# A unit's probability planes turned by four DMA transposes of 32 rows instead of one of 128

## What is computed

```python
xn = _layernorm(x, ln_gamma, ln_beta)
q = (xn @ w_q).reshape(B, SQ, NUM_HEADS, DIM_HEAD)
k, v = jnp.split(context @ w_kv, 2, axis=-1)        # context: 32 x 1500 x 128
...
scores = jnp.einsum('bqhd,bkhd->bhqk', q * SCALE, k)
attn = jax.nn.softmax(scores, axis=-1)
out = jnp.einsum('bhqk,bkhd->bqhd', attn, v).reshape(B, SQ, INNER)
out = out @ w_out + b_out
return out * jnp.tanh(gate[0])
```

## Time and profile before

| | us |
|---|---|
| median of 3 runs | 2121.29 (2121.03 to 2125.9) |
| the profiled execution, its own time | 2123.42 |
| its span, first to last instruction | 2121.6 |
| first and last issue of a transpose of this stage | 716.8, 1909.5 |

### The profile page before, as it was taken

One profiled execution on the slowest core, in us unless ns is written; L12 is line 12 of the kernel. 1 busy time (PEld: TensorE's weight loads), 2 busy tenths in 40 slices (PEclk: granted clock), 3 DMA queues, 4 the chain that ended last, 5 costly groups with the idle time before them and its releaser, 6 DMA issues. The chain is left out here.

```text
span 2121.6 us, 32242 instructions
## 1 busy us (share of the span) xinstructions
PE 1753.3 (83%) x9613; PEld 1229.7 (58%) x9613; DVE 1557.0 (73%) x2744; ACT 1153.5 (54%) x1804; POOL 821.0 (39%) x687
## 2 busy tenths in 40 slices
PE   4877886999844589989988988998898898884997
PEld 3554555888712446656655665665565566453886
DVE  4884775787755478778777877877777787775887
ACT  2432222776621566666666665666666576563453
POOL 4650111233333463444346345434533634411233
PEclk9987998899956799999999999999999999997998
DMA  5102774000000499899989989998998998882000
GB/s 203 50 0 94 292 287 189 2 1 0 1 0 30 99 197 193 182 189 188 188 185 192 195 176 189 188 193 187 191 192 170 199 192 183 180 167 87 1 9 10
DMA packets 722858, 290.11 MB, mean 137 GB/s; under 512 B 700892, under 2 KB 705020, under 8 KB 722044
## 3 DMA queue, kind: packets, MB, share of 16 engines
q1 hardware_dynamic: 722796, 289.36, 59.9%
HBM read 112.24 MB, written 0.92 MB: 53 GB/s over the span
## 5 line engine op out<-in xcount | busy, mean ns | idle before, releaser
L2147 DVE TENSOR_REDUCE xa_negmax<-xa_psum 128x1 f32<-128x1500 f32 x224 | 385.4, 1720 | 219.2 <-PE xa_psum L2055 219.2
L2265 ACT ACTIVATE xa_h<-xa_psum,xa_rinv 128x1000 f16<-128x1000 f32 x448 | 372.1, 881 | 236.1 <-DVE xa_rinv L2154 144.1
L2162 DVE SCALAR_TENSOR_TENSOR xa_h<-xa_psum,xa_rinv,xa_h 128x500 f16<-128x500 f32 x672 | 452.8, 729 | 55.3 <-ACT xa_h L2265 55.3
L2253 ACT ACTIVATE xa_psum<-xa_psum,xa_negmax 128x1500 f32<-128x1500 f32 x224 | 332.6, 1485 | 195.0 <-DVE xa_negmax L2147 195.0
L2053 PE MATMUL xa_psum<-xa_c_hi,xa_q_hi 128*128 128x500 f32 x672 | 293.2, 436 | 143.9 <-DVE xa_h L2162 134.7
L2073 PE MATMUL xa_psum<-xa_prT,xa_n_hi 128*128 128x512 f16 (+1 forms) x768 | 278.1, 362 | 5.5 <-DMA xa_prT<-xa_h 3.2
L2074 PE MATMUL xa_psum<-xa_prT,xa_n_hi 128*128 128x512 f16 (+1 forms) x768 | 274.4, 357 | 0.0
L2075 PE MATMUL xa_psum<-xa_prT,xa_n_lo 128*128 128x512 f16 (+1 forms) x768 | 273.0, 356 | 0.0
L2055 PE MATMUL xa_psum<-xa_c_hi,xa_q_lo 128*128 128x500 f32 x672 | 271.3, 404 | 0.0
L2054 PE MATMUL xa_psum<-xa_c_lo,xa_q_hi 128*128 128x500 f32 x672 | 270.5, 403 | 0.0
L2053 PEld LDWEIGHTS xa_psum<-xa_c_hi,xa_q_hi 128*128 128x128 f32 x672 | 131.5, 196 | 231.5 <-DVE xa_h L2162 183.9
(11 more groups left out here) (296 smaller groups left out, 3373.5 us busy)
## 6 DMA issues: line engine op xcount, KB each, us to landing
ctxN<-in_ctxP SPq DMA_DIRECT2D x16, 1536.0 KB, 9.3
xa_ctxP<-in_ctxP SPq DMA_DIRECT2D x32, 768.0 KB, 4.8
ctxT<-in_ctxT SPq DMA_DIRECT2D x16, 1500.0 KB, 6.3
xa_ctxT<-in_ctxT SPq DMA_DIRECT2D x32, 750.0 KB, 4.7
xa_prT<-xa_h SPq DMA_TRANSPOSE x224, 5.5
up<-in_F_up SPq DMA_DIRECT2D x1, 2048.0 KB, 9.2
down<-in_F_down SPq DMA_DIRECT2D x1, 2048.0 KB, 13.3
gate<-in_F_gate SPq DMA_DIRECT2D x1, 1024.0 KB, 4.9
```

The costliest lines, as they stand in the source:

```text
L2147: nc.vector.tensor_reduce(negmax[:, s % 2, :], psum[:, bank:bank + 3, 0:W], AX.XY, ALU.max, negate=True)\
L2162: nc.vector.scalar_tensor_tensor(h[:, H_SLOT[s], 1, a:z], psum[:, bank + j, 0:W], rinv[:, s % 2, :], h[:, H_SLOT[s], 0, a:z], ALU.mult, AL ...
L2253: nc.scalar.activation(psum[:, bank:bank + 3, 0:W], psum[:, bank:bank + 3, 0:W], ACT.Exp, bias=negmax[:, s % 2, :], accum_out=rs[:, s % 2, ...
L2265: nc.scalar.activation(h[:, H_SLOT[s], 0, a * W:z * W].rearrange("p (a c) -> p a c", c=W), psum[:, bank + a:bank + z, 0:W], ACT.Identity, ...
```

## The change

The tile `prT` gets a further dimension: instead of 24 blocks of 128 columns a slot now holds, for each of the `RG` = 4 quarters of the unit's rows, 24 blocks of 32 columns. Each quarter is turned by a DMA transpose of its own, from 32 partitions of `h` into one run of 24 x 32 elements per partition. All four add 16 to the same semaphore, so whoever waited for 16 now waits for 64. The value matmuls read, for each of 512 (or 384) columns, the same elements in the same order as before, now as 16 (or 12) runs of 32 columns.

```diff
+    RR = 32
+    RG = 128 // RR
...
-        prT = sb("prT", [128, 2 * GA + UPS - GA, 2 * KT, 128], fp16)
+        prT = sb("prT", [128, 2 * GA + UPS - GA, RG, 2 * KT, RR], fp16)
...
-                sp.dma_start_transpose(prT[:, P_SLOT[s], :, :], h[:, H_SLOT[s], :, :].rearrange("p a c -> p (a c)"))\
-                    .then_inc(transposed[s], 16)
+                for r in range(RG):
+                    sp.dma_start_transpose(prT[:, P_SLOT[s], r, :, :],
+                                           h[r * RR:(r + 1) * RR, H_SLOT[s], :, :].rearrange("p a c -> p (a c)"))\
+                        .then_inc(transposed[s], 16)
...
-                        pe.wait_ge(transposed[s], (i + 1) * 16)
-                out = psum[:, 6, 0:128 * m].rearrange("p (a b) -> p a b", a=m)
+                        pe.wait_ge(transposed[s], (i + 1) * 16 * RG)
+                out = psum[:, 6, 0:128 * m].rearrange("p (a g b) -> p a g b", a=m, g=RG)
...
-                    ph, pl = (prT[:, s0:s0 + m, x * KT + kt, :] for x in range(2))
+                    ph, pl = (prT[:, s0:s0 + m, :, x * KT + kt, :] for x in range(2))
...
-                    act.wait_ge(transposed[s - 3], (i + 1) * 16)
+                    act.wait_ge(transposed[s - 3], (i + 1) * 16 * RG)
                 elif not first:
-                    act.wait_ge(transposed[max(x for x in range(NU) if H_SLOT[x] == s)], i * 16)
+                    act.wait_ge(transposed[max(x for x in range(NU) if H_SLOT[x] == s)], i * 16 * RG)
```

## The result

The changed kernel takes 2391.85 us (median, 2390.8 to 2396.2) against 2123.60 in the same runs: a ratio of 1.126, interval 1.1238 to 1.1283. It is slower, as forecast, but by 268 us and not by the 119 us of the prediction; the time is inside the range of 2118 to 2450. The profiled execution has a span of 2394.4 us.

The account below looks back on a forecast made before the run. A ring of waits bounds the stage, with 12.7 us of SP queue slack per iteration. Four transposes fill the queue: 7.9 us more per iteration, 126 over 16, on 2121.6 us; 2240 taken, range 2118 to 2450.

Parts of the forecast that it names:

- the slack: SP queue: its own waits, 12.7 us of a 75.5 us iteration, 0.9 us per unit, as cover for added hold.
- The chain at the iteration's end: Unit 12's transpose delays ScalarE's next unit 0; the change adds 2.5 us, period 77.4, not added to the full queue.
- (a): SP queue: four 32-row transposes hold 1.22 us each, 5.03 per unit instead of 3.6; period 82.8, 126 us in all.
- (b): Landing of a unit's transposes: a small one after 2.8 us, all four after 6.6 instead of 5.5, 1.1 later.
- (c): Value matmuls reading prT in runs of 32 columns instead of 128: a dozen more breaks, taken at nothing.
- (d): Waits, context loads, DMA data and TensorE's clock, granted 0.96 to 0.97 in the stage: nothing further counted.
- The sum: Whole kernel: 2121.6 us span plus 126 gives 2247.6; with 1.16 us per piece 2195; 2240 taken.
- no fixed part: SP queue: hold proportional to data, 0.90 us per piece, 3.75 per unit, queue not full; 2126 us, chance 0.12.
- faster transposes: DMA stream: 32-row transposes fed at 290 GB/s instead of 215, chain 1.8 us shorter; about 2092 us, chance 0.10.
- The third: SP queue: hold partly by 24 column groups; 1.42 us per piece gives about 2427, 2.02 about 2960; chance 0.20.

## Why the prediction was wrong in size

- **What bounds the kernel, and the slack:** right. The chain at the iteration's end, with units 12 and 0 in one slot, was worth 5 us per iteration when it was taken away; the queue's 12.7 us of waits were used up by four pieces of either kind. That an added hold under 0.9 us per unit costs nothing but the chain's price fits the run with 96 and 32 rows, where that price was 3.2 us per iteration.
- **(a) the hold of a piece** is the step that failed. The prediction put it at 1.22 us, 5.03 per unit. The first piece has 1.25, the others 1.5, a unit 5.83. The prediction divided the data part by four, and so took the feed rate of 215 GB/s for granted at any number of rows, and counted no time between two pieces. At 32 rows the rate is about 155, and a piece with the change to the next takes 1.5 us, more than the queue's own 1.28; with that the stream sets the hold, and no longer the instruction. With the measured sizes its own sum comes out: 14 x (5.83 - 3.6) = 31.2 us; a unit behind a load is held 0.6 us longer than others (6.42 against 5.83) instead of 1.4, which takes off 4 x 0.8 = 3.2; 62.8 + 31.2 - 3.2 = 90.8 us against 91.5 measured. For the pieces by columns, with the same 3.2: 14 x (5.21 - 3.6) = 22.5, 62.8 + 22.5 - 3.2 = 82.1, measured 82.1 (1215.9 to 1298.0). That part (a) hit 1.28 us with its 1.22 there is partly luck: for halves the same formula gives 2.0, and 1.4 to 1.8 were measured.
- **(b) the latency:** 2.8 us from issue to landing was forecast for a piece, 3.6 measured with 32 rows and 2.8 with 128 rows and a quarter of the columns. The same failed step. That the full queue rules and the chain isn't added was right: the four slots of h, which shorten the chain, won nothing in the changed kernel.
- **(c) the matmuls' runs at nothing:** right, as the run with the reading pattern alone shows. **(d) the clock:** granted 0.89 in the iteration instead of 0.96 to 0.97. It was lower where TensorE waited longer for the low part: 1.00 with 4.6 us of such waits (four slots), 0.97 with 7.6 (before), 0.89 with 16 to 18 (changed). TensorE's busy time grew by 4 us per iteration, and its waits hid that: the queue's sum gives the period to within 1 us, which leaves little room for a cost of its own.
- **The sum** with these sizes would have been 15.9 to 16.7 us x 16 = 254 to 267 instead of 126; 268 measured.
- **The rivals:** "no fixed part" fell by the pieces by columns (5.21 us per unit, not 3.75), "faster transposes" by the rate, which went down. The third asked whether the cost goes by groups of columns, and its price for a hold of 1.42 us, with 5.8 us per unit and 2427 in all, is nearer to the result than the forecast; but its reason is not the one: 64 and 32 rows have one rate, and 96 and 128 the other. What it got right is that a piece with fewer rows is not a fourth of a whole one. The row that could have warned was not in the trace of before, since that kernel has no transpose of fewer than 128 rows.
- **The rule of the Trainium skill** (DMA: Bandwidth & Descriptors, section Rules for kernel authors) not to split a transfer by partition halves: the runs agree, and more strongly than the rule says. Two halves by partitions cost 7.6%, two halves by columns nothing (1.076 and 0.9997).
- **The figures of the Trainium skill** (the same page, section Latency and other measured facts) for transposes, 261 GB/s and roughly 350 to 400: neither was seen. One of 128 rows went at 215, and at 290 behind a load; a destination in one run and one in 24 runs took the same time.

Still open is why 64 and 32 rows are fed at about 155 GB/s. It isn't a limit of the engines on such pieces (281 and 288 GB/s behind a load), and it isn't the destination's layout; where between 64 and 96 rows the rate changes, and why, wasn't tried further.

## To carry over

A DMA transpose holds its queue for a large part of its time, so sum up the queue per iteration and compare its own waits with what is added. Under them most of it is covered, though not all (0.8 us per unit against 0.9 still cost 2.4%); above them more buffers don't help. Then look at what sets the hold: where the instruction itself is the longer part, its time is paid; where the stream of the piece ahead is, even 195 us of added instructions cost only 34. If a transpose must be split, split it by columns and keep the 128 rows. And where slots are handed out by s modulo n in a loop whose length n does not divide, look at the wrap: one more slot was worth 3.6% here.

## What was not expected of the hardware

- A transpose between tiles of SBUF moved 215 to 219 GB/s with 128 or 96 source rows and 152 to 158 with 64 or 32; behind a load, with a backlog, 281 to 290 at 128, 64 and 32 rows.
- A transpose holds the SP queue for at least 1.21 to 1.23 us, however small it was here; a plain copy 0.35 to 0.43, but 1.3 to 1.7 for the context loads behind transposes of 64 rows.
- Two transposes of half the columns hold the queue 3.2 us together, less than the 3.6 of one.
- Each further transpose adds 32 packets of the DMA engines: 722,396 under 512 bytes in the changed kernel, 700,892 before, for 672 more instructions.
